# Causal attention with filler matmuls on eight cores: the last pair's queries and keys in pieces of 512 tokens, fillers in halves of columns and spread further, masks first on VectorE

## The reference

```
xn = layernorm(x)
q, k, v = xn Wq, xn Wk, xn Wv        # 16 heads of 64; rotary embedding on q and k
s = (softmax(causal(q k^T / 8)) v) Wo
w1, w2 = dequantised fc1 (1024 x 4096), fc2 (4096 x 1024), groups of 128
h = layernorm(xn) * gamma + beta
f = xn + 0.5 * (silu(h w1 + b1) w2 + b2)
out = x + s * silu(f)
```

## Time and profile before

| | us |
|---|---|
| median of 3 runs | 1048.45 (1047.56 to 1053.14) |
| profiled execution, its own time | 1056.29 |
| span of its slowest core (core 2) | 1054.7 |
| spans of all cores | 1037.3 to 1054.7 |
| attention on core 2, first scores to first fc1 matmul | 94 to 539 |

### The profile page before, as it was taken

How to read it: one execution, slowest core, us unless ns; L and a number is a source line. 1 busy time by engine, 2 the same in 40 slices (tenths; PEclk the granted TensorE clock), 3 DMA queues, 4 the chain that set the end, 5 groups by cost and what they waited for, 6 DMA issues and landing times.

```text
span 1054.7 us, 14998 instructions; the slowest of 8 cores (1037.3 to 1054.7 us)
## 1 busy us (share of the span) xinstructions
PE 940.3 (89%) x5380; PEld 417.9 (40%) x5465; DVE 421.7 (40%) x668; ACT 490.6 (47%) x632; POOL 18.9 (2%) x42
## 2 busy tenths in 40 slices
PE   2567899989899889977799989899999999999997
PEld 1344333433443335322234434344444444444443
DVE  4555556566645665465710111100013333333333
ACT  6562677777787767778863323344310000000000
POOL 1000000000000000000000000000000000000000
PEclk9989999999999999997899999999999999999999
DMA  9905886557674656567249999965384243414111
GB/s 244 271 20 142 174 235 173 188 134 204 177 206 149 162 165 185 159 197 188 78 131 206 244 257 281 255 143 139 100 270 167 85 150 130 150 51 150 58 63 41
DMA packets 89289, 171.89 MB, mean 163 GB/s; under 512 B 7920, under 2 KB 45952, under 8 KB 87936
## 3 DMA queue, kind: packets, MB, share of 16 engines
q1 hardware_dynamic: 81168, 161.93, 51.9%
q0 software_dynamic: 8048, 8.98, 6.6%
HBM read 133.72 MB, written 37.76 MB: 163 GB/s over the span
## 4 chain that ended last, share of the span: by engine, by line
PE 68%; ACT 8%; DMA 7%; issue 6%; DVE 6%; SPq 4%; POOL 0%; DVEq 0%; ACTq 0%; POOLq 0%
PE ps L1036 21%; PE ps L977 14%; PE ps L795 11%; PE ps L347 6%; PE ps L745 5%; PE ps L1007 5%; ACT pb L766 5%; PE ps L386 5%; SPq L60 4%; DMA y_spill<-yst 3%; DMA wv<-wv 3%; DVE raw L356 1%; ACT linv L813 1%; DVE swp L474 1%; DVE o_fm L822 1%
## 5 line engine op out<-in xcount | busy, mean ns | idle before, releaser
L766 ACT ACTIVATE pb<-ps,negub 128x1024 bf16<-128x1024 f32 (+1 forms) x320 | 299.1, 982 | 99.4 <-PE ps L745 96.2
L977 PE MATMUL ps<-xn,w1t 128*128 128x512 bf16 x1003 | 223.0, 381 | 10.2 <-ACT yst L988 8.5
L988 ACT ACTIVATE yst<-ps,b 128x512 bf16<-128x512 f32 x128 | 84.6, 688 | 146.2 <-PE ps L977 84.4
L977 PEld LDWEIGHTS ps<-xn,w1t 128*128 128x128 bf16 x1024 | 99.8, 98 | 133.2 <-issue 15.5
L1051 ACT ACTIVATE tf<-tf 128x512 f32<-128x512 f32 x32 | 20.1, 630 | 257.9 <-DVE tf L1047 257.9
L347 PE MATMUL ps<-xn,wqk 128*128 128x512 bf16 x414 | 110.7, 387 | 7.1 <-DVE nm L436 3.1
L1036 PE MATMUL ps<-w2a,ybuf 128*128 128x512 bf16 x502 | 114.7, 379 | 0.5
L745 PE MATMUL ps<-qk,qk 64*128 64x512 bf16 (+3 forms) x640 | 99.7, 363 | 17.2 <-ACT pb L766 16.3
L1036 PE MATMUL ps<-w2b,ybuf 128*128 128x512 bf16 x489 | 112.6, 379 | 0.6
L795 PE MATMUL ps<-pb,v_tm 128*64 128x512 bf16 (+3 forms) x640 | 93.8, 369 | 20.4 <-DVE pb L777 14.5
L795 PE MATMUL ps<-pb,ones 128*64 128x512 bf16 (+3 forms) x640 | 89.9, 359 | 0.0
(11 more groups left out here) (86 smaller groups left out, 596.3 us busy)
## 6 DMA issues: line engine op xcount, KB each, us to landing
dqi<-fc_q SPq DMA_DIRECT2D x64, 512.0 KB, 5.8
dqs<-fc_scales SPq DMA_DIRECT2D x64, 512.0 KB, 7.3
y_spill<-yst SPq DMA_DIRECT2D x32, 512.0 KB, 7.7
ybuf<-y_spill SPq DMA_DIRECT2D x7, 2048.0 KB, 9.8
w_deq<-dqo SPq DMA_DIRECT2D x48, 256.0 KB, 2.7
xbuf<-x SPq DMA_DIRECT2D x16, 512.0 KB, 13.1
w1t<-w_deq SPq DMA_DIRECT2D x32, 256.0 KB, 6.7
xt<-x SPq DMA_DIRECT2D x16, 512.0 KB, 4.0
```

Of the source, the lines that this page charges most:

```text
L766: tok = SC.tick(lambda e: e.activation(fap(p, [[512, 2], [1, n]], offset=off), fap(z, [[512, 2], [1, n]], offset=off), AF.Exp, bias=negub[ ...
L977: fn = (lambda k, fc, f, tg: lambda e: e.matmul(ring[k], w1t[f % 4][:, 128 * fc:128 * (fc + 1)], xn[:, S * fc + 512 * tg:S * fc + 512 * (t ...
L988: t_ring[k] = SC.tick((lambda k, f, tg: lambda e: e.activation(yst[f % 3][:, 512 * tg:512 * (tg + 1)], ring[k], AF.Silu, bias=b1[:, f:f + ...
```

## The change

- `unit` and `v_unit` issue each matmul as two, one for each 64 columns of the array.
- Pair 7's queries and keys are computed 512 tokens at a time (query, then key), each quarter with its own copies, squares, products and sum (`quarter7`, `products7`), norm, rows and broadcast (`norm7`, `rows7`, `bc7`). Its scores wait for their quarter alone, and its exponentials use a bound for each group of queries (`negub7`), the running maximum over the quarters so far.
- The order of fillers is new, fillers reach to step 144 instead of 133, and steps of pair 0 weigh 1.15 times as much.
- In a step masks are issued first, then the scaling, then what was put off.
- Ropes are put off by 2 steps for pair 1 (3 before) and 3 for pairs 5 and 6 (5 before). The first norm of a pair comes at position 42 instead of 38.
- `g2_rep` has a place of its own and is loaded at step 100; `make_h` runs in steps 148 to 155, a block in each.

```
-                fn = (lambda e: e.matmul(p, w[:, 128 * fc:128 * (fc + 1)],
-                                         xn[:, S * fc + 512 * tg:S * fc + 512 * (tg + 1)],
-                                         start=(fc == 0), stop=(fc == NCH - 1)))
+                for r in (0, 64):
+
+                    fn = (lambda r: lambda e: e.matmul(
+                        p[r:r + 64, :], w[:, 128 * fc + r:128 * fc + r + 64],
+                        xn[:, S * fc + 512 * tg:S * fc + 512 * (tg + 1)], start=(fc == 0), stop=(fc == NCH - 1),
+                        tile_position=(0, r), skip_group_check=True))(r)
+                    if (fc, r) != (NCH - 1, 64):
+                        PE.do(fn)
...
-                if tg == 3:
+                if m == NP - 1:
+                    quarter7(j, tg)
+                elif tg == 3:
                     swap(m, j)
                     square(m, j)
-                    later(3 if m == 1 else 5, lambda: rope(m, j))
+                    later(2 if m == 1 else 3 if m >= 5 else 5, lambda: rope(m, j))
...
-                fn = (lambda e: e.matmul(
-                    z[:, 256 * u:256 * (u + 1)], xn[:, S * fc + 128 * t:S * fc + 128 * (t + 1)],
-                    wv[p][:, 256 * fc:256 * (fc + 1)], start=(fc == 0), stop=(fc == NCH - 1)))
+                for r in (0, 64):
+                    fn = (lambda r: lambda e: e.matmul(
+                        z[r:r + 64, 256 * u:256 * (u + 1)], xn[:, S * fc + 128 * t + r:S * fc + 128 * t + r + 64],
+                        wv[p][:, 256 * fc:256 * (fc + 1)], start=(fc == 0), stop=(fc == NCH - 1),
+                        tile_position=(0, r), skip_group_check=True))(r)
...
+        def quarter7(j, tg):
+            lo, hi = 512 * tg, 512 * (tg + 1)
+            SP.wait(t_raw[(NP - 1, j, tg)], t_rope[(NP - 2, j)])
+            for a, b in ((0, 32), (32, 0), (64, 96), (96, 64)):
+                t_s7[tg] = SP.dma(sl_s7[tg], swp[j][a:a + 32, lo:hi], raw[j][b:b + 32, lo:hi])
+            VE.wait(t_sqf[0], t_raw[(NP - 1, j, tg)])
+            t_sq7[(tg, j)] = VE.tick(lambda e: e.tensor_mul(
+                sq[:, 512 * j:512 * (j + 1)], raw[j][:, lo:hi], raw[j][:, lo:hi]))
+            if j == 1:
+                later(3, lambda: products7(tg))
...
-        order = [("v", 1, range(0, 4)), ("q", 1, None), ("q", 2, None), ("v", 1, range(4, 8)), ("q", 3, None), ("q", 4, None),
-                 ("v", 2, range(8)), ("q", 5, None), ("q", 6, None), ("v", 3, range(8)), ("q", 7, None)]
+        order = [("v", 1, range(0, 4)), ("q", 1, None), ("q", 2, None), ("v", 1, range(4, 6)),
+                 ("q", 3, None), ("v", 1, range(6, 8)), ("q", 4, None), ("v", 2, range(0, 6)),
+                 ("q", 5, None), ("v", 2, range(6, 8)), ("q", 6, None),
+                 ("v", 3, range(0, 6)), ("t", 0, None), ("t", 1, None),
+                 ("v", 3, range(6, 8)), ("t", 2, None), ("t", 3, None)]
...
+            elif what == "t":
+                extra.append((at_pos + 22, (0.5, (lambda m: lambda: norm7(m))(m))))
+                extra.append((at_pos + 27, (0.1, (lambda m: lambda: rows7(m))(m))))
+                extra.append((at_pos + 34, (0.1, (lambda m: lambda: bc7(m))(m))))
+                for j in range(2):
+                    units += unit(NP - 1, j, m)
+                at_pos += 16
...
-                    kinds.append((m, qg, c, w + (5.5 if c == 0 else 0.5 if c == 1 else 0.0)))
-        last_fill = 20 * (NP - 1) - 7
+                    w += 5.5 if c == 0 else 0.5 if c == 1 else 0.0
+                    kinds.append((m, qg, c, 1.15 * w if m == 0 else w))
+        last_fill = 144
...
+            if prev and prev[2] >= 2 * prev[1]:
+                for kt in (2 * prev[2], 2 * prev[2] + 1):
+                    mask(prev[0], prev[1], kt)
+            for fn in at_next:
+                fn()
+            at_next.clear()
             step()
...
-            if s == ns - 20:
+            if s == 100:
                 load_g2()
-            if ns - 18 <= s < ns - 2 and (s - ns + 18) % 2 == 0:
-                make_h((s - ns + 18) // 2)
+            if ns - 12 <= s < ns - 4:
+                make_h(s - ns + 12)
```

More of the change, by code:

```diff
@@ L136, in build_nc @@
     negub = const("negub", NP, F32, 4)
+    nm7 = const("nm7", 4, F32, 4)
+    run7 = const("run7", 4, F32, 4)
+    negub7 = const("negub7", 4, F32, 4)
     def region(size):
@@ L204, in build_nc @@
         sl_s0 = [slot(f"sS0{i}") for i in range(4)]
+        sl_s7 = [slot(f"sS7{i}") for i in range(4)]
         sl_th = slot("sTH")
@@ new lines, in products7 @@
+        def products7(tg):
+            heavy[0] = True
+            lo, hi = 512 * tg, 512 * (tg + 1)
+            VE.wait(t_s7[tg], t_last_s[NP - 3])
+            toks = []
+            for j in range(2):
+                VE.do((lambda j: lambda e: e.tensor_mul(swp[j][:, lo:hi], swp[j][:, lo:hi], sin_t[:, lo:hi]))(j))
+                toks.append(VE.tick((lambda j: lambda e: e.tensor_mul(
+                    raw[j][:, lo:hi], raw[j][:, lo:hi], cos_t[:, lo:hi]))(j)))
+            for j in range(2):
+                VE.wait(toks[j])
+                t_rope7[tg] = VE.tick((lambda j: lambda e: e.tensor_add(
+                    qb[(NP - 1) % 2][j][:, lo:hi], raw[j][:, lo:hi], swp[j][:, lo:hi]))(j))
+            t_rope[(NP - 1, 1)] = t_rope7[tg]
@@ new lines, in norm7 @@
+        def norm7(tg):
+            b = side_bank()
+            PE.wait(t_sq7[(tg, 0)], t_sq7[(tg, 1)])
+            for j in range(2):
+                fn = (lambda j: lambda e: e.matmul(
+                    ps[3][32 * j:32 * (j + 1), 512 * b:512 * (b + 1)], hsel[:], sq[:, 512 * j:512 * (j + 1)],
+                    start=True, stop=True, tile_position=(0, 32 * j), skip_group_check=True))(j)
+                if j == 0:
+                    PE.do(fn)
+                else:
+                    t_sqf[0] = PE.tick(fn)
+            VE.wait(t_sqf[0])
+            t_nm7[tg] = VE.tick(lambda e: e.reduce_max(nm7[0:64, tg:tg + 1], ps[3][0:64, 512 * b:512 * (b + 1)],
+                                                       axis=AX.X))
+            f_free[b] = t_nm7[tg]
@@ new lines, in rows7 @@
+        def rows7(tg):
+            b = side_bank()
+            PE.wait(t_nm7[tg])
+            tok = PE.tick(lambda e: e.transpose(ps[3][0:1, 512 * b:512 * b + 64], nm7[0:64, tg:tg + 1],
+                                                idn_f[0:64, 0:64]))
+            VE.wait(tok)
+            new = run7[0:1, 0:2] if tg == 0 else run7[0:1, 2:4]
+            tok = VE.tick(lambda e: e.reduce_max(
+                new, ps[3][0:1, 512 * b:512 * b + 64].rearrange("p (a b) -> p a b", b=32), axis=AX.X))
+            f_free[b] = tok
+            VE.wait(tok)
+            if tg > 0:
+                tok = VE.tick(lambda e: e.tensor_max(run7[0:1, 0:2], run7[0:1, 0:2], run7[0:1, 2:4]))
+                VE.wait(tok)
+            tok = VE.tick(lambda e: e.tensor_scalar(
+                nm2[0:1, 2:3], run7[0:1, 0:1], run7[0:1, 1:2], 1e-18, ALU.mult, ALU.max))
+            SC.wait(tok)
+            tok = SC.tick(lambda e: e.activation(nm2[0:1, 3:4], nm2[0:1, 2:3], AF.Ln))
+            SC.wait(tok)
+            tok = SC.tick(lambda e: e.activation(nm2[0:1, 2:3], nm2[0:1, 3:4], AF.Exp, scale=0.5,
+                                                 bias=ln8[0:1, 0:1]))
+            VE.wait(tok)
+            t_stb7[tg] = VE.tick(lambda e: e.tensor_scalar(
+                stb[0:1, 0:1], nm2[0:1, 2:3], 1.0, -1.0, ALU.add, ALU.mult))
@@ L491, in build_nc, with bc7 @@
+        def bc7(tg):
+            b = side_bank()
+            PE.wait(t_stb7[tg])
+            tok = PE.tick(lambda e: e.matmul(fb[b][:, 0:1], ones_row[0:1, :], stb[0:1, 0:1], start=True, stop=True))
+            VE.wait(tok)
+            t_neg7[tg] = VE.tick(lambda e: e.tensor_copy(negub7[:, tg:tg + 1], fb[b][:, 0:1]))
+            f_free[b] = t_neg7[tg]
         load_wv(0)
@@ L646, in build_nc @@
                     units += v_unit(m, t2)
-            at_pos += 64 if what == "q" else 8 * len(part)
+                at_pos += 8 * len(part)
+        extra.sort(key=lambda x: x[0])
         fill = []
@@ L737, in scores @@
                 PE.wait(t_rope0[qg])
+            elif m == NP - 1:
+                PE.wait(t_rope7[qg])
             else:
@@ L840, in load_g2 @@
         def load_g2():
-            GP.wait(t_row[0], t_rope[(NP - 1, 1)])
+            GP.wait(t_row[0])
             t_g2[0] = GP.dma(sl_gr, g2_rep[:], bass.AP(g2_d, 0, [[0, 128], [1, S]]))
@@ L950, in build_nc @@
             if f == 0:
-                GP.wait(t_o[31], t_ds[n_att - 1], t_ds[n_att - 2], t_ds[n_att - 3])
+                GP.wait(t_o[31], t_ds[n_att - 1], t_ds[n_att - 2], t_ds[n_att - 3], t_h[NCH - 1])
                 SP.wait(t_att, t_ds[n_att - 1], t_ds[n_att - 2], t_ds[n_att - 3])
@@ L998, in load_xt @@
         def load_xt(t):
-            SP.wait(t_fin.get(t - 2), t_h[NCH - 1])
+            SP.wait(t_fin.get(t - 2), t_h[NCH - 1], t_rope7[3])
```

22 lines of the change are left out of this document (10 added, 12 removed).

## The result

Over 18 runs the changed kernel takes 1056.52 us in the median, the kernel before 1049.91. The ratio, which leaves out executions in which one die ran at a lower granted clock, is 1.0056, 95% interval 1.0029 to 1.0083: slower by 0.6%, where 1.7% faster was forecast, outside the range of 1016 to 1044. The profiled execution has a span of 1055.1 us (core 1; all cores 1039.5 to 1055.1).

What follows compares the result with a forecast made beforehand. PE was taken to bound the first 130 attention steps, ACT the last 30. Halves -10, spreading -12, masks -8 and added costs +12 sum to -18 us: 1030.5 us against the median 1048.45, range 1016 to 1044.

Steps and rivals of the forecast that it cites:

- Pair 1's sines: Attention, pair 1's ropes one step earlier: DVE waits for swapped copies, 1 us for each sine, +2 us, bounds 0 and 5.
- DVE becomes what PE waits for: Rival: masks give only 2, dense scaling costs 4, sines and maxima 5 and 9; 1047 us, at half 1039; chance 0.13.
- Spreading fillers: Attention: fillers to step 144 instead of 133 leave the PE-bound part and cover waits; -12 us, bounds 8 and 15.
- so 1.5 less than now: Steps 130 to 140: 20 us of attention work plus 10 of fillers make 30 us, against 31.5 now.
- near 473.5: Sign in the profile after: the last filler matmul, in step 140, stands near 473.5 us.
- Masks first, -8: Attention: masks, then scaling, ahead of ropes remove 8 of PE's 14.5 us of mask waits; bounds 2 and 14.5.
- Halves, -10: First 130 steps: half-column fillers save a 0.10 us shape change in 104 steps, -10 us; small full-array matmuls add 4.
- Preparation, +0.5: Preparation before attention: half value units cost 8 x 0.2 us on a PE with 43 us idle, taken as +0.5 us.
- Quarters +4: Pair 7: four norms, rows and broadcasts, with waits for DVE's maxima, add 4 us; bounds 2 and 9.
- dense scaling +1.5: End of attention: xn's scaling in 8 steps instead of 16 puts DVE behind at group 2's masks; +1.5 us, bounds 0 and 4.
- shape change isn't saved: Rival: values after half fillers still wait for the array to empty, so the -10 falls away; 1040.5 us, chance 0.08.
- weight loads: Rival: half value fillers' two loads go one after the other, 0.22 us a pair, 42 us more; 1072 us, chance 0.07.

Runs made afterwards that it cites:

- e5: Changed kernel with ropes put off as before (3 steps for pair 1, 5 for others) and fillers to step 133 instead of 144; ratio to kernel before 0.9976.
- e1: Changed kernel with ropes put off as before, 3 steps for pair 1 and 5 for all others; ratio to kernel before 0.992.
- e3: Kernel before with only masks, then scaling, issued ahead of what was put off; ratio to kernel before 0.9914.
- e11: Kernel before with only masks and scaling put first, repeated on another chip; ratio to kernel before 0.9909.
- e7: Changed kernel with ropes put off as before and xn's scaling spread as before, every second step from 142; ratio to kernel before 0.9969.
- e2: Kernel before with only fillers in halves of columns (edits of `unit` and `v_unit`); ratio to kernel before 0.9977.
- e6: Kernel before with halves of columns and masks first, nothing else; ratio to kernel before 0.993.
- e13: Changed kernel with early ropes, dequantisation from step 24 on and weight loads waiting for a later event, away from pair 1's copies; ratio to kernel before 1.0029.
- e9: Changed kernel with bulk loads held back by steps: query and key weights by 4, dequantisation loads up to 3 after a copy; ratio to kernel before 1.007.

## Why the prediction was wrong, by its own steps

- **Pair 1's sines, "2; bounds 0 and 5": the term that failed most.** With pairs 5 and 6, priced at nothing, the line cost 8.4 us of attention, 7.5 of them in steps 0 to 20, and some 14 in all; alone, 16.9 and 15. The prediction gave 1 us to each of the two sines for a step of lateness and looked at no landing time. But a sine waits for its own copy. Pair 1's took 6.7 us in the kernel before already (core 1, where the median of all 56 is 2.5), and 8.4 in the changed one, in a stretch with full DMA engines, where PE's cover is two banks. Moving the rope also moved the loads, as a step with a rope puts its dequantisation off and the two come together just ahead of the next copies (133.54 and 135.08). It is the rival "DVE becomes what PE waits for" by its place, above the 5 us that it gave to sines.
- **Spreading fillers, -12: measured 0 (e5).** The step that failed is "so 1.5 less than now". The stretch from 461.5 to 493.0 that I took for steps 130 to 140 runs from step 128 into step 141; those ten steps take 25.2 us, and 28.9 after. The 45 weights of the sum are the twelve steps 130 to 142. They take 30.4 us before and 28.9 in e5, both without fillers, and with them 37.3 after and 38.4 in e1, where the sum had 30: it added 10 us of fillers to 20 us of work on PE, but the stretch is 28.9 long without them. Steps 140 to 144 take 16.6 us, 4.8 more than before, and the last filler stands at 500.3 us (core 1), not near 473.5. Waits for bounds weren't covered: the broadcast of a bound still holds PE for 2.30 us at 478.53, behind the cast of another filler, and for 1.52 at 502.22 (above). In attention 10 us of fillers cost about 10 us at either place; what the ratio leaves open is said at e5.
- **Masks first, -8: right alone**, 9 us by the ratio, with 8.6 of the 14.5 us of waits gone (e3, e11). In the changed kernel only 4.1 of them are gone; 2.1 of what is left stand at step 152 (532.69) and go when the scaling is spread (e7).
- **Halves, -10 with 4 for small matmuls: the shape change is saved as forecast, half the time isn't.** On core 1 from 155 to 430 us, 48 borders of query fillers went from 0.309 to 0.216 and 25 of value fillers from 0.203 to 0.109, 6.8 us; in the same window the second pair of 512-column scores starts later behind the first, by 2.0 us over 59 cases, narrower ones by some 1.8, and waits for ACT went from 2.4 to 5.1. PE came earlier to a score whose bank ACT had not read yet. Attention fell by 4.6 where 6 were forecast, the preparation gave 1.4 back; the time fell by 2.4. That ACT is the taker is read from these rows, and no run isolates it.
- **Preparation, +0.5: 1 to 2.6.** Its last value fillers run at a mean clock of 0.74 on core 1, where the kernel before had 0.81 on the same core. Over 85 to 94 us the clock is 0.62 to 0.81 on the eight cores after; before it is 1.00 on six of them, in e2 (halves alone) on three, in e11 (masks alone) on six:

```profile
85.00:94.00 9.00, 6.08 (x66) 3.87 (x62) 4.14 (x9) 0.69 (x3) 0.00 (x0) 0.74 0.62 112
```

  So it seems to go with the halves, which no run isolates; why the lower level (1.2 GHz) was granted for part of the stretch stays open.
- **Quarters +4 and dense scaling +1.5.** e6 to e5, which differ in these, in the order of the fillers and in smaller things (weights of pair 0, first norm, load of g2), is +5.8 in attention. The scaling shows at its place (+2.2) and costs nothing as a whole (e7), so nearly all is the quarters, the order and the smaller things. They weren't parted.
- The rivals "shape change isn't saved" and "weight loads" are refuted by the timeline. Of the Trainium skill's rules weighed there (TensorEngine Tiling (Array Packing)), the one of Key Properties on mode changes agrees with the trace; by the one of Restrictions and Gotchas on the fast weight load the price was between 0 and 42 us, and it is 0 here, as halves keep the pace of 0.109 a pair.

The sum by the runs, in attention: halves and masks -13.3, quarters, order and scaling +5.8, spreading +1.2, early sines +8.4: +2.1, and the preparation +2.6. The measured end of attention is 4.7 later.

## What to carry to other kernels

Before work that waits for a small transfer is moved forward, look at the landing time of that very transfer and at what the DMA engines carry in those 10 us. A median over all transfers hides it. Another queue moved the wait from one sine to another here; loads that could go elsewhere took it away. A stretch with idle time on PE doesn't take filler work for nothing: 10 us of it made twelve steps 9.5 us longer here (e5 to e1). Check a stretch's ends by instruction before reasoning on its length. An order of two operations on one in-order engine was worth more than every reshaping here.

## What the runs showed of the hardware

- Changing column halves within one shape costs nothing at 0.216 or 0.109 us a pair; a change of shape costs 0.09 to 0.10 us.
- Four 128 KB copies inside the chip land in 2.3 us in the median where the DMA engines were idle before them (DMA share 0.01 in 130 to 136.8 us, core 1 of e13), and in 10.1 us behind and beside loads of 2.5 MB (same core after).
- The untouched fc1 has a spread of its own. From its first matmul to the end a core takes 504 us, in the profiles at hand up to 524 in some cores (516 before, 504 in all of the changed kernel's, 519 in e13's, 524 in e9's), where DMA is full and PE idles (core 5 of e13 in two stretches):

```profile
600.00:640.00 40.00, 35.63 (x157) 15.53 (x156) 6.13 (x5) 12.31 (x20) 0.00 (x0) 0.96 0.97 254
640.00:680.00 40.00, 34.61 (x146) 14.64 (x145) 6.13 (x5) 11.12 (x19) 1.06 (x2) 0.91 0.95 267
```

  Core 0 of e13 has DMA shares of 1.00 and 0.95 in the same two stretches and PE busy 39.8 of 40 us, so a full DMA alone doesn't tell the cores apart; the cause stays open. The metric is the slowest core, so some gains in attention don't reach it: e13 wins 7.2 us in attention over the changed kernel and 3 in the ratio.
